# An S4D convolution and a LoRA linear layer in one kernel: x1 made in place by a predicated copy, strips gathered by GpSimd, B split per tile

## The reference, cut to what matters

```
K    = 2 * Re( sum_n Ct[h,n] * exp(dtA[h,n] * l) )        # one filter per head, 512 taps
y    = causal_conv(x, K) + x * D                          # per head
x1   = x + where(position < length[batch], y, 0)
out  = x1 + x1 @ W.T + bias + (x1 @ A[id].T) @ B[id].T    # id per batch row; rank 16, 32 adapters
```

## Time and profile before

| | us |
|---|---|
| median of 3 runs | 223.27 (223.0 to 224.22) |
| the profiled execution | 224.23 |
| its span, first to last instruction | 222.5 |
| TensorE busy | 196.1 (88%) |
| VectorE busy | 172.7 (78%) |
| ScalarE busy | 114.4 (51%) |
| GpSimd busy | 90.8 (41%) |

### The profile page before, as it was taken

The page is one execution under the profiler, slowest core; times in us unless marked ns, Lnnn a source line. Parts: engine busy times, 40 slices in busy tenths (PEclk is TensorE's granted clock), DMA queues, the critical chain, the costliest instruction groups (busy, mean ns, idle before and its releaser), DMA issues.

```text
span 222.5 us, 4340 instructions
## 1 busy us (share of the span) xinstructions
PE 196.1 (88%) x1046; PEld 167.4 (75%) x1046; DVE 172.7 (78%) x374; ACT 114.4 (51%) x329; POOL 90.8 (41%) x144
## 2 busy tenths in 40 slices
PE   0065799999899889989899999999999999999993
PEld 0043699988798779977688888888888888888882
DVE  4787649978799966668999888878888888887641
ACT  2738134336364343156766766666666666666310
POOL 4820000005297075408665455545454555454300
PEclk9997589999999999999999999999999999999998
DMA  5995999899999999714566776767676767663412
GB/s 134 309 379 147 354 417 384 266 403 411 409 404 408 416 391 409 256 46 144 180 225 248 214 245 183 242 192 217 208 228 189 230 197 233 192 217 108 175 49 94
DMA packets 21537, 56.46 MB, mean 254 GB/s; under 512 B 3410, under 2 KB 3858, under 8 KB 21394
## 3 DMA queue, kind: packets, MB, share of 16 engines
q1 hardware_dynamic: 18370, 47.78, 60.0%
q0 software_dynamic: 2560, 8.39, 12.5%
q10 hardware_dynamic: 592, 0.13, 0.3%
HBM read 45.64 MB, written 10.65 MB: 253 GB/s over the span
## 4 chain that ended last, share of the span: by engine, by line
PE 66%; DVE 15%; DMA 11%; issue 4%; ACT 3%; ACTq 1%; POOL 0%; DVEq 0%; SPq 0%; POOLq 0%
PE y_ps L921 37%; PE z_ps L884 15%; DMA strip<-k_pad 7%; PE z_ps L909 6%; PE y_ps L930 3%; PE y_ps L931 3%; DVE z_all L716 3%; DMA k_pad<-k_sb 2%; DVE xp L710 1%; ACT xp L433 1%; DVE ee L682 1%; DMA par<-params 1%; DVE gg L677 1%; PE k_ps L870 1%; DVE work L667 1%
## 5 line engine op out<-in xcount | busy, mean ns | idle before, releaser
L921 PE MATMUL y_ps<-w_hi,xp 128*128 128x512 f32 x256 | 85.1, 393 | 0.0
L884 PE MATMUL z_ps<-xp,strip 128*128 128x512 f32 (+3 forms) x384 | 67.8, 335 | 4.3 <-DMA strip<-k_pad 4.2
L884 PEld LDWEIGHTS z_ps<-xp,strip 128*128 128x128 f32 x384 | 62.0, 202 | 10.4 <-DMA strip<-k_pad 6.2
L921 PEld LDWEIGHTS y_ps<-w_hi,xp 128*128 128x128 f32 x256 | 48.1, 188 | 9.7
L921 PE MATMUL y_ps<-w_lo,xp 128*128 128x512 f32 x128 | 50.3, 393 | 0.0
L402 POOL CAST ag<-a_hl 128x128 fp32r x64 | 24.4, 383 | 50.3 <-PE z_ps L909 34.0
L407 POOL DMA_INDIRECT b_hl<-b_tab,b_idx x32 | 38.6, 1208 | 9.6 <-issue 9.1
L516 ACT ACTIVATE ag<-a_hl 128x64 fp32r x128 | 25.6, 249 | 19.7 <-issue 19.4
L433 ACT ACTIVATE xp<-z_all 128x512 fp32r<-128x512 f32 x32 | 19.8, 627 | 28.2 <-PE z_ps L884 25.7
L803 DVE TENSOR_TENSOR a_raw<-y_ps,bias_sb 128x512 f32<-128x512 f32 x32 | 22.0, 689 | 14.3 <-issue 7.2
L716 DVE TENSOR_TENSOR z_all<-z_ps,mask 128x512 f32<-128x512 f32 (+2 forms) x33 | 22.1, 670 | 10.9 <-PE z_ps L884 10.6
(11 more groups left out here) (107 smaller groups left out, 170.0 us busy)
## 6 DMA issues: line engine op xcount, KB each, us to landing
strip<-k_pad SPq DMA_DIRECT2D x32, 512.0 KB, 10.0
z_all<-x_conv SPq DMA_DIRECT2D x16, 512.0 KB, 10.6
x_t<-x_tile SPq DMA_DIRECT2D x32, 256.0 KB, 2.7
out<-a_raw SPq DMA_DIRECT2D x32, 256.0 KB
x_t<-b_rows SPq DMA_DIRECT2D x1, 1024.0 KB, 7.2
a_raw<-a_t SPq DMA_DIRECT2D x2, 512.0 KB, 9.2
w_sb<-w_t SPq DMA_DIRECT2D x2, 512.0 KB, 10.4
b_tab<-w_hi SPq DMA_DIRECT2D x2, 512.0 KB, 10.8
```

The lines of the kernel that those rows point to most:

```text
L884: last = nc.tensor.matmul(z_ps[:, h % ZS, m * P:L], strip[:, h % SS, m * P:(m + 1) * P, t], xp[:, h % XS, 0:LC - m, e, :], start=(n == 0), ...
L921: last = nc.tensor.matmul(y_ps[:, s % TS, :], xp[:, s % XS, c, e, :], w[:, c, :], start=(n == 0), stop=False)
```

## The change

1. x is loaded once, in natural order, and the strip's rows run the other way: each starts one tap earlier than the one before. Such descending starts are given by a list of offsets (`s_idx`), so that the strips are now loaded by an indirect DMA of GpSimd. `k_pad` becomes one tensor per group.
2. The row that adds D adds D + 1, so that the product gives x + y; `head` is a predicated copy: where the mask is set the result goes over x in `z_all`, elsewhere x stays. The second load of x, the VectorE addition and their buffers fall away; `x1_hi` and `x1_remainder` read `z_all`.
3. B's table is no longer split and stored. GpSimd gathers raw rows of B for each tile, ScalarE rounds them (`b_rounded`), VectorE takes the remainder on 64 of the 128 partitions (`b_remainder`).
4. GpSimd's order: 32 strips, with four steps of the split of A between them; 4 gathers of B; the A copies of tiles 0 and 1; then the identity and the split of W by twos. `SPLIT_W` moves from heads 25 to 28 to heads 28 to 31.
5. `keep_warm` runs 14 and 10 products instead of 6 and 6; group 2 is multiplied after head 0 instead of 1, group 4 after 14 instead of 13. One pair of x less is loaded ahead.

```diff
-PRE = 7
-X_AT = {1: 7, 3: 8, 6: 9, 8: 10, 10: 11, 14: 12, 16: 13, 19: 14, 21: 15}
-A_AT, W_AT = {5: 0, 7: 1}, {11: 0, 13: 1}
-TAB_HI_AT, TAB_LO_AT = {18: 0, 20: 1}, {22: 0, 23: 1}
+PRE = 6
+X_AT = {0: 6, 2: 7, 4: 8, 6: 9, 10: 10, 12: 11, 16: 12, 18: 13, 19: 14, 21: 15}
+IDS_AT = 3
+A_AT, W_AT = {8: 0, 14: 1}, {20: 0, 23: 1}
 BIAS_AT = 24
-XT_AT = {25: 0, 26: 1, 27: 2, 28: 3}
-SPLIT_B = {14: 0, 15: 1, 16: 2, 17: 3}
-SPLIT_A = {18: 0, 19: 1, 20: 2, 21: 3}
-SPLIT_W = {25: 0, 26: 1, 27: 2, 28: 3}
-K_AFTER = {2: 1, 3: 7, 4: 13}
+SPLIT_A = {18: 0, 20: 1, 23: 2, 25: 3}
+SPLIT_W = {28: 0, 29: 1, 30: 2, 31: 3}
+LOW_A = {20: 0, 22: 1, 25: 2, 27: 3}
+K_AFTER = {2: 0, 3: 7, 4: 14}
 STEPS_AT = {3: (4, 5, 6, 7, 8, 9), 4: (10, 11, 12, 13, 14, 15)}
+WARM_0, WARM_1 = 14, 10
...
-            sp.dma_start(b_raw[:, :, :], b_rows).then_inc(b_in, 16)
+            for k, (h0, h1) in enumerate(GROUPS):
+                sp.dma_start(k_pad[k][:, 0:P, :].rearrange("h (o p) e -> h o (p e)", o=2),
+                             zero[0:h1 - h0, :].unsqueeze(1).to_broadcast((h1 - h0, 2, P))).then_inc(pad_stored, 16)
...
             for n in range(2, PRE):
                 load_pair(n)
...
+            sp.wait_ge(k_stored, 16)
+            for h in range(BIAS_AT + 1):
+                if h:
+                    sp.wait_ge(conv_done, h)
                 if h in X_AT:
                     load_pair(X_AT[h])
...
+            g.iota(s_idx[:, :], pattern=[[2 * PAD, G]], base=2 * P, channel_multiplier=-2).then_inc(idx_made, 1)
...
-            for n in range(NW):
+            def low_a(n):
...
-            for c in range(LC):
-                pool.wait_ge(w_in[c // 2], 16)
-                d = w_sb[:, c, c * P:(c + 1) * P]
-                g.tensor_tensor(d, d, eye[:, :], ALU.add).then_inc(w_eye, 1)
-            pool.wait_ge(w_eye, LC)
-            pool.wait_ge(tab_lo_stored, 32)
-            for n in range(LC):
-                split_w(n)
+            def load_strip(k, h):
+                (h0, h1), s = GROUPS[k], h % SS
+                rows = bass.AP(tensor=k_pad[k].tensor, offset=0, ap=[[2 * L, (h1 - h0) * PAD // L], [1, 2 * L]])
+                g.indirect_dma_start(out=strip[:, s, :, :].rearrange("p l e -> p (l e)").bitcast(F32), out_offset=None,
+                                     in_=rows, in_offset=bass.IndirectOffsetOnAxis(ap=s_idx[:, h - h0:h - h0 + 1], axis=1)
+                                     ).then_inc(strip_landed[s], 16)
+            pool.wait_ge(idx_made, 1)
+            pool.wait_ge(pad_stored, 16 * NG)
+            for k, (h0, h1) in enumerate(GROUPS):
+                pool.wait_ge(k_stored, 16 * (k + 1))
+                for h in range(h0, h1):
+                    if h >= SS:
+                        pool.wait_ge(conv_done, h + 1 - SS)
+                    load_strip(k, h)
+                    if h in LOW_A:
+                        low_a(LOW_A[h])
...
-                g.indirect_dma_start(out=b_hl[:, t % BS, :].bitcast(F32), out_offset=None, in_=b_tab,
+                g.indirect_dma_start(out=b_raw[:, t % BR_S, :], out_offset=None, in_=b_rows,
                                      in_offset=bass.IndirectOffsetOnAxis(ap=b_idx[:, t:t + 1], axis=0)
-                                     ).then_inc(b_landed[t % BS], 16)
...
             pool.wait_ge(idx_ready, 1)
             pool.wait_ge(ids_ready, 1)
+            for t in range(BR_S):
+                gather_b(t)
             pool.wait_ge(a_split, NW)
-            pool.wait_ge(w_split, NW)
-            for t in range(NT):
-                if t >= TS:
-                    pool.wait_ge(h_done, t + (1 - TS))
+            for t in range(TS):
+                gather(t, t)
+            for c in range(LC):
+                pool.wait_ge(w_in[c // 2], 16)
+                d = w_sb[:, c, c * P:(c + 1) * P]
+                g.tensor_tensor(d, d, eye[:, :], ALU.add).then_inc(w_eye, 1)
+                if c % 2:
+                    split_w(c - 1)
+                    split_w(c)
+            for t in range(TS, NT):
+                pool.wait_ge(h_done, t + (1 - TS))
                 gather(t, t % TS)
-                if t >= BS:
-                    pool.wait_ge(y_done, t + (1 - BS))
-                gather_b(t)
+                if t + TS < NT:
+                    pool.wait_ge(b_split, t + (1 - TS))
+                    gather_b(t + TS)
...
-                if h in SPLIT_B:
-                    n = SPLIT_B[h]
...
                 if h in SPLIT_W:
                     n = SPLIT_W[h]
                     act.wait_ge(w_eye, n + 1)
-                    act.wait_ge(tab_hi_stored, 32)
...
-                act.wait_ge(x1_done, t + 1)
                 if not first:
                     act.wait_ge(base_done, t + (1 - XS))
-                act.activation(xp[:, s % XS, :, 0, :], in_chunks(x_t[:, s % XT, :]), ACT.Copy).then_inc(xhi_done, 1)
+                act.activation(by_head(xp[:, s % XS, :, 0, :]), z_rows(t), ACT.Copy).then_inc(xhi_done, 1)
+            def b_rounded(t, s, lap):
+                act.wait_ge(b_landed[s % BR_S], 16 * (lap + 1))
+                if not isinstance(t, int) or t >= BS:
+                    act.wait_ge(y_done, t + (1 - BS))
+                act.activation(b_hl[:, s % BS, :], b_raw[:, s % BR_S, :], ACT.Copy).then_inc(b_hi_done, 1)
...
                 h_rounded(i + 1, b, known and i + 1 < TS)
+                if not known or i + 2 < NT:
+                    b_rounded(i + 2, s + 2, lap + (s + 2) // BR_S)
...
-            act.activation(by_head(xp[:, 0, :, 0, :], 0, EARLY), by_head(in_chunks(x_t[:, 0, :]), 0, EARLY),
-                           ACT.Copy).then_inc(xhi_early, 1)
             gather(0, 0)
-            act.wait_ge(x1_done, 1)
-            act.activation(by_head(xp[:, 0, :, 0, :], EARLY, NH), by_head(in_chunks(x_t[:, 0, :]), EARLY, NH),
-                           ACT.Copy).then_inc(xhi_done, 1)
+            act.wait_ge(factors, 2 * NG)
+            b_rounded(0, 0, 0)
+            act.wait_ge(z_masked, EARLY)
+            act.activation(by_head(xp[:, 0, :, 0, :], 0, EARLY), z_rows(0, 0, EARLY), ACT.Copy).then_inc(xhi_early, 1)
+            act.wait_ge(z_masked, NH)
+            act.activation(by_head(xp[:, 0, :, 0, :], EARLY, NH), z_rows(0, EARLY, NH), ACT.Copy).then_inc(xhi_done, 1)
+            act.wait_ge(z_masked, NH + 1)
+            x1_hi(1, 1, True)
             gather(1, 1)
             h_down(0, 0)
-            x1_hi(1, 1, True)
             h_rounded(0, 0, True)
             x1_hi(2, 2, True)
             gather(2, 0)
+            b_rounded(1, 1, 0)
...
                 dve.wait_ge(conv_done, h + 1)
-                V.tensor_tensor(z_all[:, h, :, b0:b1], in_chunks(z_ps[:, h % ZS, :])[:, :, b0:b1], mask[:, :, b0:b1],
-                                ALU.mult).then_inc(z_masked, 1)
+                V.copy_predicated(z_all[:, h, :, b0:b1], mask[:, :, b0:b1].bitcast(I32),
+                                  in_chunks(z_ps[:, h % ZS, :])[:, :, b0:b1]).then_inc(z_masked, 1)
...
-            def x1_of(t, s, lap):
-                dve.wait_ge(xt_landed[s % XT], 16 * (lap + 1))
-                xt = by_head(in_chunks(x_t[:, s % XT, :]))
-                V.tensor_tensor(xt, xt, z_rows(t), ALU.add).then_inc(x1_done, 1)
...
-                V.tensor_tensor(xp[:, s % XS, :, 1, :], in_chunks(x_t[:, s % XT, :]),
-                                xp[:, s % XS, :, 0, :].bitcast(F32), ALU.subtract).then_inc(xlo_done, 1)
+                V.tensor_tensor(by_head(xp[:, s % XS, :, 1, :]), z_rows(t), by_head(xp[:, s % XS, :, 0, :].bitcast(F32)),
+                                ALU.subtract).then_inc(xlo_done, 1)
+            def b_remainder(t, s):
+                dve.wait_ge(b_hi_done, t + 1)
+                V.tensor_tensor(b_hl[BR:P, s % BS, :], b_raw[BR:P, s % BR_S, :], b_hl[BR:P, s % BS, :].bitcast(F32),
+                                ALU.subtract).then_inc(b_split, 1)
...
-                if there(i + 4):
-                    x1_of(i + 4, s + 4, lap + (s + 4) // XT)
...
+                if there(i + 2):
+                    b_remainder(i + 2, s + 2)
...
             dve.wait_ge(bias_in, 16)
-            dve.wait_ge(z_masked, NH + 1)
-            x1_of(1, 1, 0)
+            b_remainder(0, 0)
             h_masked(0, 0)
             x1_remainder(1, 1)
-            x1_of(2, 2, 0)
             h_remainder(0, 0)
             x1_remainder(2, 2)
-            x1_of(3, 3, 0)
+            b_remainder(1, 1)
...
-            keep_warm(6)
+            keep_warm(WARM_0)
             group(1)
-            keep_warm(6)
+            keep_warm(WARM_1)
...
-                pe.wait_ge(b_landed[s % BS], 16 * (lap + 1))
+                pe.wait_ge(b_split, t + 1)
...
             pe.wait_ge(z_masked, EARLY)
-            pe.wait_ge(w_split, NW)
             pe.wait_ge(xlo_early, 1)
             tile_h(0, 0, True)
+            pe.wait_ge(w_split, NW)
...
-        "x_conv": g["x"].reshape(NB, NH, LC, P)[..., ::-1].transpose(3, 1, 2, 0).reshape(P, NH, L),
```

(4 more changed lines are left out.)

119 lines of the change are left out of this document (33 added, 86 removed).

## The result

| | before | after |
|---|---|---|
| median | 223.13 us (222.97 to 224.22, 4 runs) | 228.72 us (227.3 to 230.27, 4 runs) |
| profiled execution / its span | 224.23 / 222.5 | 228.64 / 226.3 |
| time outside the span, all runs | 1.70 to 1.82 | 2.30 to 3.27 |

The change makes the kernel slower: ratio 1.0243, 95% interval [1.0195, 1.0291]. The forecast was 224.2 in a range of 218.5 to 228.5; the median lies 4.5 us above the forecast and just outside the range. The side was right (slower was given the largest chance), the size was not.

The account below looks back on a forecast made before the run. TensorE, busy for 88% of the span, was taken to bound the kernel, with transfers the limit from 60 to 90 us. Terms -2.3 - 4.9 + 7.9 + 0.3 = +1.0 on 224.23 gave 225.2, median 224.2, range 218.5 to 228.5.

Parts of the forecast that it names:

- Opening: Span start to head 2: fewer transfers ahead of the filter store and a longer warm-up, -2.3 us.
- Heads 2 to 25: Convolution's middle: TensorE binds by a small margin at 1.97 us a head, -4.9 us, bounds 0 to -5.5.
- two readings of the queues: Heads 2 to 25: GpSimd's own queue lets strips pass x, -4.9 in full; one queue for all, nearer -3.
- third rival: Slower: GpSimd's strips come no faster than 2.17 us each, the -4.9 is lost, 229.1 or 228; chance 0.17.
- The predicated copy: In the heads, replacing the multiply: 0 us, VectorE being off the path; 0.69 us a copy taken.
- Tail: Head 25's end to first tile: GpSimd's order stalls head 29 by 5.6 us, clock loss 2.5; +7.9 us.
- bounds of 3.5 to 7.8: Tail: limits of TensorE's stall before head 29, 3.5 us with gathers of 0.96, 7.8 with gathers at 1.6.
- Tiles: First tile to span end: ScalarE's extra rounding fits under 3.70 us a tile; first two tiles cost, +0.3 us.
- h chain: Tiles: claimed to have over 3 us in hand when ScalarE gets one more rounding of 0.62 us.
- signs of being wrong: No gap at head 29, strip waits between heads 4 and 25, copy over 1.1 us, tiles over 3.72 us.
- The frame: Outside the span: median taken 1.0 us below the profiled execution, so 225.2 became 224.2.
- first rival: Faster: gain of 7.2 us before T stands, stall 3.5, clock holds; -3.6 us, 219.7; chance 0.30.

Follow-up runs that it names:

- experiment 6: Kernel after with 6 and 6 warm-up products, as before the change, instead of 14 and 10: 229.75 us, ratio 1.0288.
- experiment 9: Kernel after with GpSimd's four steps for A moved behind the strips 28 to 31: 229.93 us, ratio 1.0289.
- experiment 5: Kernel after with the strips loaded by SyncE's queue, rows ascending, instead of GpSimd's indirect DMA (output differs): 231.31 us, ratio 1.0346.
- experiment 7: Kernel after with a multiply by the mask in place of the predicated copy (output differs): one run, 229.13 us.
- experiment 1: Kernel after with GpSimd adding the identity to W right behind strips 29 and 31, ahead of B's gathers: 226.92 us, ratio 1.0135.
- experiment 4: Kernel after with identity added to W early, B rounded before A copies, B's remainder before h's, GpSimd's A steps one strip later: 222.66 us, ratio 0.9935.
- experiment 8: Kernel of experiment 4 with the pairs of x asked for earlier: 224.3 us, ratio 1.0015 against the kernel before.

## Why the prediction was wrong, step by step

**Opening: right.** -2.3 forecast and measured. Group 1 came at 19.41 (forecast 0.7 later than 18.78), group 2 at 26.12 (forecast 26.0). The clock was up for head 0; experiment 6 shows what it would have been otherwise.

**Heads 2 to 25: the failed step.** The prediction said of GpSimd's four steps for A that they "lie at heads 20 to 27 and are caught up by strip 30". They were caught up, but too late. I counted GpSimd's work against 1.97 us a head, which is its throughput. What mattered was the slack of one strip: 9.85 us of the five heads less a landing time of 8.7, that is 1.15 at the best. An A step of 1.3 to 1.5 us behind a wait for ScalarE of 2.07, which my working did not look for, is more than that. Of the missing 2.8 us, 2.2 stand from head 15 to head 26 (23.84 us from 56.93 to 80.77, against 11 x 1.97). From head 15 to T, experiment 9 gets back 1.2 of 2.0 by moving only these steps, experiment 5 all 2.0 by taking the strips off GpSimd. The other half of the step, that TensorE binds and not the transfers, held with strips by SyncE, where 14 heads ran at 1.97. With strips by GpSimd it was a near thing: the landing of 8.7 us in the median (10.0 before) became 10.2 for the strips issued from 64 to 72 us, over the 9.85 of five heads, and it is this that leaves no room for a late strip. Of the prediction's two readings of the queues neither came out whole. What the landing of GpSimd's strips owes to its queue and what to x and W beside them, no run separates, and the last 0.8 us stay open. The third rival, strips by GpSimd at 2.17 a head, is partly what happened (2.09 net: 50.1 us for 24 heads), but in the main by its place in GpSimd's order, not by a dearer descriptor step: a strip took 1.05 us to issue on the mean, under the 1.21 I used.

**The predicated copy: right**, nothing on the path, 0.73 us a copy where 0.69 was taken (experiment 7, one run).

**Tail: the mechanism right, the size too large.** Forecast +7.9, measured +5.6. The gap was 4.04 us instead of 5.6: the strip and the gathers came at 1.25 a piece instead of 1.37 and the four copies of A took 1.0 instead of 2.3, so that the addition was done 1.9 us earlier; the remainder for head 29, held up by GpSimd's split, gave 0.65 of it back. The gap lies in the bounds of 3.5 to 7.8 that the prediction gave, but these don't follow from its own terms: five gathers of 0.96 in place of 1.21 take 1.25 off 5.6 and leave 4.35, and 1.6 gives 7.55. The clock fell as expected, to 0.50 from 91 to 94 us, but the three heads lost 1.5 to 1.6 us (7.47 against 5.9), not 2.5. Experiment 1 takes the stop away and the clock's loss at these heads goes with it. The forecast took GpSimd's durations from the earlier trace rows, where these steps stood singly among others; in a row here they were cheaper.

**Tiles: the other failed step.** Forecast +0.3, measured +2.7. My argument was one of sums: ScalarE gets 0.62 and has room for it. It has, 58.77 of 80 us. But the new rounding was put last in ScalarE's order and its remainder last in VectorE's, right ahead of the bias, so that both became links of a loop of 3.74 us round VectorE and ScalarE. The prediction had said that "the h chain has over 3 us in hand"; that was its distance to TensorE's use, and not the way back through VectorE's bias. Nine tiles took 3.713 us each before (115.18 to 148.60) and 3.747 after; over the 26 tiles from the sixth to the last it is 96.55 us before and 97.22 after, 0.7 more. The first tile to the sixth took 18.07 us (99.21 to 117.28) against 17.12 (98.06 to 115.18), 0.95 more, where I had allowed -0.3 to 1.6 and taken 0.3. From the start of the last tile to the end of the span it took 11.8 us against 10.8, the last 1.0. That the tiles "run at more than 3.72 us each" was among the signs of being wrong, and it came. Moving two calls takes back 1.9 of the 2.7 (experiment 4) and the loop with it; most of the 0.8 that stay lies in the first tiles (17.85 us to the sixth against 17.12).

**The frame.** 0.6 us of the miss lies outside the span, and 1.1 in having carried the profiled execution's distance from the median over to the new kernel, which did not show it. Sum of the miss: 2.8 - 2.3 + 2.4 in the span, 0.6 and 1.1 outside it, 4.6 of 4.5 (the parts are rounded). That the forecast was only 4.5 us off is in part luck: the tail, sized 2.3 too large, covers as much of the two losses that were missed.

**The first rival** (faster, 219.7) had the right idea of where time lay: with the stop, the order of the tiles and the splits mended, a gain over the kernel before comes out, at 220.84 us. As a forecast of this change it failed, since it left out two of the three losses.

## What to carry to other kernels

Where an engine issues the loads that TensorE needs, judge each other step on it by the slack of a single load (time of the buffers ahead less time to landing), and count the waits inside the step, not the mean work of the engine. Where an edit adds a link to an in-order engine, walk once round the loop that the engines form through each other; a stage in which TensorE is busy all the time can still be paced by such a loop, and it shows in the chain of waits and in the distance of two equal instructions. Before a row of GpSimd's elementwise steps goes where it seems free, look for a subtraction of VectorE with two inputs in SBUF beside it on the path: here such a one ended only with the row.

## What the runs showed of the hardware that was not expected

- A VectorE subtraction of 128x480 took 4.49 us and one of 128x32 took 4.62, where 0.64 and 0.19 are usual, through four GpSimd subtractions of 4.97 and 4.91 us in all; in the experiments 1 and 4 the same subtraction took 2.81 and 1.45 and ended 0.52 us behind the row again. In these runs GpSimd did not let go between its instructions. In the kernel after it did: the remainder took 1.34 us and the second of GpSimd's two splits 1.74 instead of 1.27.
- The time outside the span was 1.70 to 1.82 us in all runs of the kernel before, and 2.17 to 3.38 in the runs of the kernels with strips by GpSimd. With strips by SyncE it was 1.72 to 3.08. So it differs with the kernel, but no run isolates what in it.
- A row of 4 KB costs GpSimd hardly more time than one of 2 KB: 128 rows took 1.05 us on the mean for the strips and 0.97 for B in the kernel after.
- The six and six warm-up products of experiment 6 left the clock at 0.50 for the head behind them; with the fourteen and ten of the kernel after, which run from 13.43 on with one filter group between them, it read 1.00 there.
- The stops of TensorE of 2.25 us (experiment 1), 3.94 (experiment 8) and 4.04 (kernel after) were each followed by 3 to 6 us at a granted clock of 0.50; that of 0.89 us in experiment 4 was not.
